# A Trainium2 kernel whose last wait, for all stores, is moved from the sync engine to TensorE

## The chip, the cores and the metric

The kernel runs on one core of one Trainium2 chip. The metric is the device time of one execution in microseconds (us). It covers the program's instructions and something around them: the profiled execution has a time of 46.19 us, and its span, from the first to the last instruction of the kernel, is 44.9 us.

## The reference

64 samples of 64 channels by 512 steps (float32) are each multiplied by one 64 by 64 matrix, picked from a table of 200 by an integer per sample, and the product is added to the sample:

```
w = weights[conditions]                      # (64, 64, 64)
out = x + einsum('bct,bcd->bdt', x, w)       # x, out: (64, 64, 512)
```

## The kernel before

Two samples lie one above the other on the 128 partitions, so there are 32 pairs of 512 columns. The pairs go through the kernel in eight turns of four pairs (1 MB in, 1 MB out a turn). The identity is added to every gathered matrix, so that one product gives `x + x @ w`.

Each engine has its own function, which only lists that engine's instructions in order.

- SyncE (`on_sync`) issues five loads (L94; turns 0, 1, 2, 3 and then 4 to 7 in one of 4 MB), waits until VectorE has moved its part of turns 0 to 2 (L96), and then issues six stores (L101), each behind waits for both engines that write `y_sb` (L98, L99): turns 0 and 1 together, 2 and 3 together, then 4, 5, 6 and 7 one by one. Every store adds 16 to the semaphore `stored` when its bytes have landed. SyncE's last instruction is L102, the wait for `stored` at 96, which is 16 times six.
- TensorE (`on_tensor`) spreads the row numbers (L140), runs ten matmuls on loaded data whose result nobody reads (L146), computes turns 0 to 2 in quadrants (L158), turn 3 with block-diagonal weights (L166), and turns 4 to 7 with the same helper in a loop of two passages (L177) of two turns each. A turn in the loop begins with waits for the data (L179) and the placed weights (L181, L182). The loop is the last thing in TensorE's program.
- ScalarE and VectorE build the weights and move each turn's two products from PSUM to `y_sb` (L117, L216), which raises `moved_by_act` and `moved_by_dve`.
- GpSimd gathers the matrices (L128) and passes the arrival of x on to TensorE (L134).

The framework puts a few instructions ahead of each engine's function, all listed under L235: a DRAIN and a semaphore event per engine, by which the engines start together, and four small memsets on GpSimd. It puts none behind the functions. What the chip does after the last instruction of an engine is in no row.

Of the kernel before, what the change touches and what calls it, by code (L numbers as in the profile page):

```python
# [7 lines left out]
def conditioned_residual_kernel(nc: bass.Bass, x: bass.AP, conditions: bass.AP, table: bass.AP, out: bass.AP):  # L8
# [26 lines left out]
    STORES = [(0, 1), (2, 3), (4, 4), (5, 5), (6, 6), (7, 7)]  # L35

    ctx = ExitStack()
    with ctx:
# [3 lines left out]
        def semaphore(name):  # L42
            return ctx.enter_context(nc.semaphore(name))
# [39 lines left out]
        stored = semaphore("stored")  # L83

        def halves(h):
            return slice(h * C, (h + 1) * C)

        def pairs_of(first, last=None):
            return slice(4 * first, 4 * (first if last is None else last) + 4)

        def on_sync(sp):
            for first, last in LOADS:
                pairs = pairs_of(first, last)
                sp.dma_start(x_sb[:, pairs, :], x[:, pairs, :]).then_inc(x_loaded[first], 16)  # L94

            sp.wait_ge(moved_by_dve, SETS + 1)  # L96
            for first, last in STORES:
                sp.wait_ge(moved_by_act, last + 1)  # L98
                sp.wait_ge(moved_by_dve, last + 1)  # L99
                pairs = pairs_of(first, last)  # L100
                sp.dma_start(out[:, pairs, :], y_sb[:, pairs, :]).then_inc(stored, 16)  # L101
            sp.wait_ge(stored, 16 * len(STORES))  # L102

        def on_scalar(act):
            act.dma_start(condition[:, :, :], conditions).then_inc(condition_loaded, 16)
# [30 lines left out]
        def on_tensor(pe):  # L136

            pe.wait_ge(one_set, 1)
            pe.wait_ge(rows_along, K)
            nc.tensor.matmul(product[0][0][:, 0, 0:1], row_along[:, :, :, :].rearrange("one h k n -> one (h k n)"),  # L140
                             one[:, :], start=True, stop=True).then_inc(rows_spread, 1)

            pe.wait_ge(x_loaded[0], 16)
            pe.wait_ge(x_loaded[1], 16)
            with pe.Fori(0, 5):
                nc.tensor.matmul(product[1][0][:, 0, :], x_sb[:, 0, 0:P], x_sb[:, 0, :], start=True, stop=True)  # L146

            pe.wait_ge(w_ready, 1)
            for turn in range(TILED):
                pe.wait_ge(x_loaded[turn], 16)  # L150
                if turn >= SETS:
                    pe.wait_ge(moved_by_act, turn - SETS + 1)
                    pe.wait_ge(moved_by_dve, turn - SETS + 1)
                for j in range(2):
                    for g in range(2):
                        n = 4 * turn + 2 * j + g
                        for h in range(PAIR):
                            product_of = nc.tensor.matmul(product[turn % SETS][h][halves(g), j, :],  # L158
                                                          w_all[halves(h), :, n], x_sb[halves(h), n, :],
                                                          start=True, stop=True)  # L160
                product_of.then_inc(multiplied, 1)

            def whole_pairs(s, x_pair):
                for j in range(2):
                    for g in range(2):
                        product_of = nc.tensor.matmul(product[s][j][:, g, :], w_diag[:, s, 2 * j + g, :],  # L166
                                                      x_pair(2 * j + g), start=True, stop=True)
                product_of.then_inc(multiplied, 1)

            pe.wait_ge(x_loaded[TILED], 16)
            pe.wait_ge(moved_by_act, TILED - SETS + 1)
            pe.wait_ge(moved_by_dve, TILED - SETS + 1)
            whole_pairs(TILED % SETS, lambda g: x_sb[:, 4 * TILED + g, :])
            pe.wait_ge(moved_by_act, LOOPED - SETS + 1)
            pe.wait_ge(moved_by_dve, LOOPED - SETS + 1)
            with pe.Fori(0, (TURNS - LOOPED) // SETS) as passage:  # L177
                for s in range(SETS):
                    pe.wait_ge(x_ahead, passage * SETS + (s + 1))  # L179

                    pe.wait_ge(placed_by_act, passage * SETS + (s + 1))  # L181
                    pe.wait_ge(placed_by_dve, passage * SETS + (s + 1))  # L182
                    whole_pairs(s, lambda g: x_sb[:, bass.ds(passage * (4 * SETS) + (4 * (LOOPED + s) + g), 1), :])

        def on_vector(dve):
            nc.vector.memset(zero[:, :], 0.0).then_inc(zero_set, 1)
# [27 lines left out]
            for turn in range(TURNS):  # L214
# [3 lines left out]
                if TILED <= turn <= LAST - SETS:  # L218
                    nc.vector.tensor_copy(w_diag[halves(1), turn % SETS, :, D:PAIR * D],  # L219
                                          w_all[halves(1), :, pairs_of(SETS + turn)].rearrange("p d n -> p n d")  # L220
                                          ).then_inc(placed_by_dve, 1)

        on_sync(nc.sync)
        on_scalar(nc.scalar)
        on_gpsimd(nc.gpsimd)
        on_tensor(nc.tensor)
        on_vector(nc.vector)

# [28 lines left out]
```

## Time and profile before

| what | us |
|---|---|
| three runs | 46.01, 46.11, 48.03 |
| median | 46.11 |
| the profiled execution's own time | 46.19 |
| its span | 44.9 |
| its own time less its span | 1.3 |

The rows further down are all of the profiled execution. Engines are PE (TensorE matmuls), PEld (its weight loads), DVE (VectorE), ACT (ScalarE), POOL (GpSimd) and SP (SyncE). A "q" behind a name is the engine's sequencer, which deals with waits, registers, branches and the issue of DMAs. The duration of a wait instruction in these rows is only its execution, once the semaphore has its value; the time before it is in the view of waits.

### The profile page before, as it was taken

How to read it: one execution, taken by the hardware profiler on the slowest of the kernel's cores; microseconds unless marked ns; L12 is line 12 of the kernel's file. 1: busy time of each engine (PE TensorE's matmuls, PEld its weight loads, DVE VectorE, ACT ScalarE, POOL GpSimd, SP SyncE). 2: the span in 40 equal slices, each digit the busy share in tenths (PEclk: the TensorE clock that was granted, in tenths of full speed). 3: DMA queues.
4: the chain of work that ended last, by engine and by line, in shares of the span. 5: the costliest groups of instructions: out<-in, count | busy, mean ns of one | idle time of the engine just before them, and what ended most of it. 6: DMA issues, size and time to landing. Idle time of an engine off the chain costs nothing.

```text
span 44.9 us, 331 instructions
## 1 busy us (share of the span) xinstructions
PE 31.0 (69%) x100; PEld 13.4 (30%) x100; DVE 15.1 (34%) x24; ACT 13.4 (30%) x16; POOL 1.6 (4%) x9
## 2 busy tenths in 40 slices
PE   0040000499999979999999699999999999920000
PEld 0040000433534144543453235344354453300000
DVE  1220000000009990758730490085086073063000
ACT  0894000000000064736710480085085071062000
POOL 4008100000000000000000000000000000000000
PEclk9999999999999999999999999999999999999999
DMA  0389999999999899999995989999998999999993
GB/s 0 81 314 431 424 431 431 424 431 431 416 438 519 372 467 467 467 467 467 438 467 248 438 380 424 409 453 438 424 424 372 409 424 424 431 424 394 402 438 153
DMA packets 1730, 17.83 MB, mean 397 GB/s; under 512 B 194, under 2 KB 194, under 8 KB 194
## 3 DMA queue, kind: packets, MB, share of 16 engines
q1 hardware_dynamic: 1584, 16.78, 89.2%
q0 software_dynamic: 144, 1.05, 5.5%
q10 hardware_dynamic: 2, 0.00, 0.0%
HBM read 9.44 MB, written 8.39 MB: 397 GB/s over the span
## 4 chain that ended last, share of the span: by engine, by line
DMA 50%; PE 31%; SPq 4%; DVE 3%; issue 1%; POOLq 0%
DMA x_sb<-x 50%; PE product L166 31%; SPq L94 4%; DVE y_sb L216 3%; POOLq L134 0%
## 5 line engine op out<-in xcount | busy, mean ns | idle before, releaser
L166 PE MATMUL product<-x_sb,w_diag 128*128 (+1 forms) x40 | 17.7, 597 | 0.4 <-POOLq L134 0.4
L216 DVE COPY y_sb<-product 128x1024 f32<-128x1024 f32 x8 | 9.8, 1224 | 12.9 <-PE product L166 10.5
L117 ACT COPY y_sb<-product 128x1024 f32<-128x1024 f32 x8 | 8.1, 1012 | 13.6 <-PE product L166 11.3
L146 PE MATMUL product<-x_sb 128*128 128x512 f32 x10 | 7.3, 907 | 5.4 <-DMA x_sb<-x 5.4
L166 PEld LDWEIGHTS product<-x_sb,w_diag 128*128 128x128 f32 x40 | 7.4, 190 | 10.5 <-issue 10.5
L158 PE MATMUL product<-x_sb,w_all 64*64 64x512 f32 x48 | 5.5, 601 | 0.3 <-DVE w_all L205 0.3
L146 PEld LDWEIGHTS product<-x_sb 128*128 128x128 f32 x10 | 2.9, 302 | 9.1 <-issue 9.1
L111 ACT COPY w_diag<-w_all 64x256 f32<-64x256 f32 x1 | 0.6, 642 | 12.3 <-DVE w_all L205 12.3
L202 DVE TENSOR_TENSOR gathered<-gathered,piece 128x64 f32<-128x64 f32 x1 | 0.3, 267 | 10.2 <-DMA gathered<-weights,table_row 10.2
L158 PEld LDWEIGHTS product<-x_sb,w_all 64*64 64x64 f32 x48 | 2.5, 200 | 3.3 <-issue 2.1
L205 DVE STREAM_TRANSPOSE w_all<-gathered 128x2048 f32<-128x2048 f32 x1 | 2.3, 2311 | 0.0
L140 PE MATMUL product<-one,row_along 1*128 1x1 f32 x2 | 0.6, 342 | 2.5 <-DVE row_along L193 2.5
L120 ACT COPY w_diag<-w_all 64x256 f32<-64x256 f32 x3 | 1.9, 633 | 0.0
L108 ACT ACT_TABLE_LOAD x1 | 1.3, 1283 | 1.3 <-PEq L235 1.3
L219 DVE COPY w_diag<-w_all 64x256 f32<-64x256 f32 x3 | 1.2, 410 | 0.1
L108 ACT COPY w_diag<-zero 64x512 f32<-64x512 f32 x2 | 1.2, 616 | 0.0
L140 PEld LDWEIGHTS product<-one,row_along 1*128 1x128 f32 x2 | 0.5, 304 | 2.5 <-issue 2.5
L128 POOL DMA_INDIRECT gathered<-weights,table_row x1 | 1.1, 1068 | 2.3 <-DVE table_row L196 2.3
L113 ACT COPY w_diag<-w_all 64x256 f32<-64x256 f32 x1 | 0.6, 642 | 0.0
L193 DVE TENSOR_SCALAR row_along<-condition 1x64 f32<-1x64 int32 x2 | 0.3, 178 | 0.8 <-DMA condition<-conditions 0.8
L209 DVE COPY w_diag<-w_all 64x256 f32<-64x256 f32 x1 | 0.4, 401 | 0.0
L196 DVE CAST table_row<-product 128x1 int32<-128x1 f32 x1 | 0.2, 158 | 0.7 <-PE product L140 0.7
(9 smaller groups left out, 1.6 us busy)
## 6 DMA issues: line engine op xcount, KB each, us to landing
x_sb<-x SPq DMA_DIRECT2D x4, 1024.0 KB, 9.3
x_sb<-x SPq DMA_DIRECT2D x1, 4096.0 KB, 22.7
out<-y_sb SPq DMA_DIRECT2D x2, 2048.0 KB, 8.0
out<-y_sb SPq DMA_DIRECT2D x4, 1024.0 KB, 5.4
condition<-conditions ACTq DMA_DIRECT2D x1, 0.2 KB
gathered<-weights,table_row POOLq DMA_INDIRECT x1, 9.8
```

Of the source, the lines that this page charges most:

```text
L94: sp.dma_start(x_sb[:, pairs, :], x[:, pairs, :]).then_inc(x_loaded[first], 16)
L108: nc.scalar.copy(w_diag[halves(h), :, :, (1 - h) * D:(2 - h) * D].rearrange("p s n d -> p (s n) d"), zero[halves(h), :].unsqueeze(2).to_br ...
L117: nc.scalar.copy(y_sb[:, 4 * turn:4 * turn + 2, :], product[turn % SETS][0][:, :, :]).then_inc(moved_by_act, 1)
L120: nc.scalar.copy(w_diag[halves(0), turn % SETS, :, 0:D], w_all[halves(0), :, pairs_of(SETS + turn)].rearrange("p d n -> p n d")).then_inc( ...
L128: nc.gpsimd.indirect_dma_start(gathered[:, :], None, table, bass.IndirectOffsetOnAxis(ap=table_row[:, 0:1], axis=0)).then_inc(w_gathered, 16)
L140: nc.tensor.matmul(product[0][0][:, 0, 0:1], row_along[:, :, :, :].rearrange("one h k n -> one (h k n)"), one[:, :], start=True, stop=True ...
L146: nc.tensor.matmul(product[1][0][:, 0, :], x_sb[:, 0, 0:P], x_sb[:, 0, :], start=True, stop=True)
L158: product_of = nc.tensor.matmul(product[turn % SETS][h][halves(g), j, :], w_all[halves(h), :, n], x_sb[halves(h), n, :], start=True, stop= ...
L166: product_of = nc.tensor.matmul(product[s][j][:, g, :], w_diag[:, s, 2 * j + g, :], x_pair(2 * j + g), start=True, stop=True)
L205: nc.vector.transpose(w_all[:, :, :], gathered[:, :].rearrange("p (d c) -> p d c", d=D)).then_inc(w_ready, 1)
L216: nc.vector.tensor_copy(y_sb[:, 4 * turn + 2:4 * turn + 4, :], product[turn % SETS][1][:, :, :]).then_inc(moved_by_dve, 1)
L219: nc.vector.tensor_copy(w_diag[halves(1), turn % SETS, :, D:PAIR * D], w_all[halves(1), :, pairs_of(SETS + turn)].rearrange("p d n -> p n ...
```

## The change

The wait for `stored` at 96 is taken out of SyncE's program, where it is the last instruction, and put at the end of TensorE's, behind the loop. Nothing else is touched.

```diff
@@ on_sync
                 pairs = pairs_of(first, last)
                 sp.dma_start(out[:, pairs, :], y_sb[:, pairs, :]).then_inc(stored, 16)
-            sp.wait_ge(stored, 16 * len(STORES))
@@ on_tensor
                     pe.wait_ge(placed_by_act, passage * SETS + (s + 1))
                     pe.wait_ge(placed_by_dve, passage * SETS + (s + 1))
                     whole_pairs(s, lambda g: x_sb[:, bass.ds(passage * (4 * SETS) + (4 * (LOOPED + s) + g), 1), :])
+            pe.wait_ge(stored, 16 * len(STORES))
```

## Rows read from the trace of the kernel before

**Rows 1.** The page's 40 slices of the span: busy tenths and granted clock

```profile
PE   0040000499999979999999699999999999920000
DVE  1220000000009990758730490085086073063000
ACT  0894000000000064736710480085085071062000
PEclk9999999999999999999999999999999999999999
DMA  0389999999999899999995989999998999999993
```

**Rows 2.** Chain that ended last, its last pieces: start us, us, what

```profile
25.55 0.03 POOLq L134
25.57 14.01 PE product L166 x32
39.58 0.02 issue
39.60 1.22 DVE y_sb L216
```

**Rows 3.** Waits of SP's queue: us in total, times, longest

```profile
SPq L99 <- DVE y_sb L216: 33.9, 6, 17.9
SPq L102 <- DMA out<-y_sb: 3.6, 1, 3.6
```

**Rows 4.** Timeline from 39 us to the end: start us, us, engine, line

```profile
39.60 1.01 ACT L117 COPY y_sb<-product 128x1024 f32<-128x1024 f32 x1 [2.42 <-PE product L166]
40.90 0.33 SPq L101 DMA_DIRECT2D out<-y_sb  x1
```

**Rows 5.** L101, the stores' issue, and its time to landing

```profile
L101 SPq DMA_DIRECT2D out<-y_sb x6: 332/332/347, 22.9 to 40.9; - x6
DMA to landing us min/median/max: 3.9/6.4/8.6
```

**Rows 6.** Wait instructions L102 (SP), L99 (SP), L182 (PE), L144 (PE): duration ns, starts

```profile
L102 SPq EVENT_SEMAPHORE  x1: 17/17/17, 44.9 to 44.9; - x1
...
L99 SPq EVENT_SEMAPHORE  x6: 17/17/28, 21.2 to 40.9; - x6
...
L182 PEldq EVENT_SEMAPHORE  x4: 51/51/51, 23.2 to 34.4; - x4
...
L144 PEldq EVENT_SEMAPHORE  x1: 51/51/51, 8.3 to 8.3; - x1
```

**Rows 7.** L177, the loop's own instructions on PE's sequencer: duration ns, first and last start

```profile
L177 PEldq FUSED_REGOPS  x2: 50/50/50, 23.1 to 28.0; - x2
L177 PEldq ALU_OP  x2: 32/32/32, 27.6 to 35.1; - x2
L177 PEldq COMPARE_BRANCH  x2: 76/142/209, 27.7 to 35.2; - x2
L177 PEldq MOVE  x1: 33/33/33, 23.0 to 23.0; - x1
```

**Rows 8.** Windows: stretch, us, busy (x instructions), granted PE clock, DMA share, GB/s

```profile
41.24:44.87 3.63, 0.00 (x0) 0.00 (x0) 0.00 (x0) 0.00 (x0) 0.00 (x0) 0.99 0.81 334
44.87:46.40 1.53, 0.00 (x0) 0.00 (x0) 0.00 (x0) 0.00 (x0) 0.00 (x0) 0.50 0.00 0
46.30:46.50 0.20, 0.00 (x0) 0.00 (x0) 0.00 (x0) 0.00 (x0) 0.00 (x0) 0.66 0.00 0
...
46.44:47.00 0.56, 0.00 (x0) 0.00 (x0) 0.00 (x0) 0.00 (x0) 0.00 (x0) 1.00 0.00 0
```

**Rows 9.** L235, the framework's opening instructions by engine: duration ns, starts

```profile
L235 POOLq EVENT_SEMAPHORE  x2: 17/17/17, 0.6 to 0.6; - x2
L235 SPq DRAIN  x1: 7/7/7, 0.0 to 0.0; - x1
L235 DVEq DRAIN  x1: 10/10/10, 0.1 to 0.1; - x1
L235 ACTq DRAIN  x1: 8/8/8, 0.1 to 0.1; - x1
L235 POOLq INC_SWDGE_SEM  x1: 31/31/31, 0.1 to 0.1; - x1
L235 POOL MEMSET const-float32-0.0<- x1: 104/104/104, 0.2 to 0.2; 128x1 f32 x1
L235 PEldq DRAIN  x1: 8/8/8, 0.3 to 0.3; - x1
L235 SPq EVENT_SEMAPHORE  x1: 17/17/17, 0.7 to 0.7; - x1
L235 PEldq EVENT_SEMAPHORE  x1: 51/51/51, 0.7 to 0.7; - x1
```

## The prediction

> **What bounds the kernel now.** I read the page's slices first. They show the DMA engines busy in nearly every slice from 3 to 39, TensorE busy up to slice 36 and idle in the last four [rows 1]. So the last part of the span belongs to the stores. The chain that ended last gives its steps: the arrival of x is passed on at 25.55 us, TensorE's products run from 25.57 to 39.58, VectorE's last copy from 39.60 to 40.82 [rows 2]. The timeline then has the last store, issued at 40.90 and done with issuing at 41.23 [rows 4], and the waits of SP's queue close it: the wait at L102 stood 3.6 us until that store had landed [rows 3], which is the landing of 3.9 us after its issue, the shortest of the six [rows 5]. L102 itself starts at 44.9 and takes 17 ns; it is the last instruction of the span [rows 6].
>
> None of this is touched. The change moves no load, matmul, copy or store, only the instruction that stands behind the last landing. It can therefore change three things: how soon that instruction runs once the last bytes are there, how long it takes, and what lies between it and the end of the measured time, about which the profile says little. I sum against the profiled execution: 46.19 us, of which 44.87 is the span and 1.32 lies around it. It is 0.08 above the median of the runs, 46.11.
>
> **How much lies behind the wait.** The windows behind the span carry no instruction, but they have a granted clock until a certain point: 0.50 from 44.87 to 46.40, 0.66 as the mean from 46.30 to 46.50, and 1.00 from 46.44 on, where nothing is recorded any more [rows 8]. For the mean of 0.66, x of the 0.20 us must be at 0.50 and the rest at 1.00: x = 0.2 * 0.34 / 0.5 = 0.136. The record ends at 46.44. The first busy instruction of the program, GpSimd's memset, starts at 0.2 to 0.25 [rows 9], and 46.44 - 0.25 = 46.19, the execution's own time. That is a fit and no proof, but I take it: all of the time outside the span lies behind the wait, 46.44 - 44.87 = 1.57 us. I call it the tail. It is an estimate, and it bounds from above what can be won, since no other cost is in reach of the change.
>
> **The change part by part.**
>
> *SP loses L102.* Its last instruction is then the issue that ends at 41.23 [rows 4], 3.6 us before the last landing [rows 3]. Whatever SP does for itself at the end of a program now lies beside the last store, which moves 334 GB/s in that stretch with all engines idle [rows 8]. It is cover of 3.63 us for a tail of 1.57, more than enough.
>
> *TensorE gets a wait.* Nothing is queued behind it in TensorE's program, and no engine waits for anything that comes after it. Its sequencer reaches it early: the loop's last ALU_OP and branch start at 35.1 and 35.2 [rows 7], while the matmuls already handed over run on to 39.58 [rows 2]. An instruction of the sequencer does not hold up matmuls in front of it, as the four waits at L182 show: the last starts at 34.4 [rows 6] in the midst of slices at 90% [rows 1]. Its cost there is nothing, hidden by the last matmuls and then by the last store. If that cover were gone it would be one instruction of 51 ns.
>
> *The wake-up.* A wait on SP takes 17 ns, on PE 51 [rows 6], so the span ends 34 ns later. How long each takes to notice a landing has no row good to a few ns. POOL's 25.55 reaches PE's matmul at 25.57 with its own 0.03 in it [rows 2]; the start releases SP and PE alike at 0.7 [rows 9]. The bounds are 0 and 0.03, and I take 0.01. Together the span gets 0.04 to 0.05 longer: 44.92.
>
> *The tail with PE as the last to arrive.* The trace doesn't show this part, so it is bounded from both sides. If the tail is the same whoever comes last, the cost is zero. If it is all SP's own work, it goes beside the last store and 1.57 is won. If it is work that each engine does for itself, PE does it more slowly: its sequencer starts MOVE, FUSED_REGOPS and a wait at 23.0, 23.1 and 23.2 [rows 6, 7], 0.1 us apart, while SP has a wait and the start of the store's issue between the copy's end at 40.82 and 40.90 [rows 2, 4], 0.04 apart. At 0.06 more an instruction, a tail of 1.57 that holds 1.57 / 0.04 = 39 of SP's instructions would be 2.3 longer. So the ends are -1.57 and +2.3. The value that I take is zero to +0.1, say +0.01, by the nearest row: at the only point where all engines meet, the start, SP and PE are released in the same tenth of a microsecond [rows 9], which speaks for a meeting that hardly depends on who it is.
>
> The sum: 46.19 + 0.034 + 0.01 + 0.01 = 46.24 on the profiled execution's scale, 46.16 on the scale of the median. I forecast 46.2, no change that can be seen; 2% of this kernel is 0.92 us, about what a measurement of it can tell from no change.
>
> One rule speaks against the change. In the opening rows the engines do not begin together: SP's DRAIN starts at 0.0, those of DVE and ACT at 0.1, PE's at 0.3 [rows 9]. The Trainium skill, page "Runtime: NRT & Kernel Launch", section "The ~15µs preamble/postamble breakdown", says that the runtime's barriers go from engine to engine and back, eight hops of 44 ns over five engines. An engine at the head of such a line that comes last pays eight hops, one at its far end four. If PE is the head, as its late start would fit, the page would make the time an estimated 4 * 44 = 176 ns longer: 46.4. The order of the starts agrees with a line of that sort, but a different amount of work ahead of the DRAINs would look the same. The same table gives the barrier behind a kernel about 1.5 us; the tail of 1.57 from the windows is that long, and no row here shows what is in it.
>
> **The rivals.**
>
> *A: the line of engines (0.3 us).* By rows alone: PE starts 0.3 after SP [rows 9]. If this order is that of a line in which word is passed on, and the last to arrive must pass it the long way, then the end is later by up to the same 0.3, so 46.5; if the line runs the other way round, earlier by as much, 45.9. For it: the stagger. Against it: at 0.7 both are released at once. Either way it is within 2%.
>
> *B: SP's own work at the end is hidden.* For it: SP has issued eleven DMAs and has their queue to look after, and it is free from 41.23. Against it: no row shows any such work, and TensorE must have an end of its own, which now comes last. If half of the tail is SP's and PE has nothing like it, 46.19 - 0.78 + 0.04 = 45.4; if all of it, 44.7. It is faster by over 2% when SP's share exceeds PE's by 0.96 us, some 60% of the tail.
>
> *C: TensorE's own end is dearer, the other side.* In the kernel before, TensorE is through with its program by 39.6 at the latest [rows 2] and does whatever it has to do at the end beside the last copies and the last store, at a granted clock of 0.99 to 1.00 [rows 1, 8]. In the kernel after it does so behind the last landing, with nothing beside it. The price is 0.06 us for each instruction that both have, by the pace above. If half of the tail is such work, 20 instructions, 1.2 us: 47.4; if all, 48.5. It decides from 15 instructions on (15 * 0.06 = 0.9). The clock is at 0.50, which is 1.2 GHz, in the stretch behind the span, after TensorE has been idle since 39.58 [rows 2, 8]; if the sequencer's pace hung on it, each instruction would cost yet more. For it: the pace of PE's sequencer, 51 ns against 17. Against it: the common release at the start.
>
> *D: the move does nothing.* Should the end of the program wait for the DMA queue on SP in any case, SP stays the last and PE's wait runs beside it: 46.19 to 46.24.
>
> **How the numbers follow.** The forecast has 0.40, with a range of its own of 46.0 to 46.5. A has 0.15, B 0.22, C 0.18, D 0.05. Of B somewhat more than half, 0.12, is beyond 2% (below 45.2); of C half, 0.09, is beyond 47.0. That leaves 0.79 within 2%. The range that should hold the time 8 times in 10 reaches well into B and C: 45.1 to 47.1, with about 0.11 below and 0.08 above.
>
> **What would show it right or wrong.** The last instruction of the changed profile must be a semaphore event of 51 ns on PE's sequencer, and its wait must name the stores as its releaser; its length is from 35.3 to 44.9, over 9 us, and costs nothing. SP's last row must be the issue at 40.9. Everything up to 40.9 must be as before, the last landing again 3.9 us after its issue; the span must be 44.9. If the difference between the execution's own time and its span stays at 1.3, forecast and D hold; 1.0 or 1.6 is A; 0.9 or less is B; 1.9 or more is C. The forecast would be wrong if the own time moved by more than 0.3 while the span did not, for then the tail depends on who comes last; it would be wrong in another way if the last store itself landed at another time, which none of the cases has a reason for.

## The result and the profile after

| | before | after |
|---|---|---|
| median us | 46.05 | 46.34 |
| runs, lowest to highest us | 18, 45.81 to 48.03 | 18, 46.18 to 46.60 |
| profiled execution: own time, us | 46.19 | 46.43 |
| its span, from the trace, us | 44.87 | 44.84 |
| own time less span, us | 1.32 | 1.59 |

The ratio of after to before is 1.0066 with a 95% interval of 1.0051 to 1.0081. The changed kernel is slower by 0.3 us: well within 2%, but clear of the noise. Executions far above their fellows, like the one of 48.03 us, are left out of every ratio. The profiled execution's span is even 0.03 us shorter than before.

The page of the changed kernel begins with its span and its slices; these lines answer to [rows 1]:

```profile
span 44.8 us, 331 instructions
...
PE   0040000499999369999999699999999999920000
...
PEclk9999999999999999999999999999999999999975
DMA  0679999999999799999995999899998999999993
```

The pattern at the end is that of before: DMA up to slice 39, TensorE idle in the last four. Only the granted clock is lower in the last two slices. The timeline from 40 us on shows the same end as [rows 2, 4], 0.04 to 0.05 us earlier throughout:

```profile
39.56 1.01 ACT L116 COPY y_sb<-product 128x1024 f32<-128x1024 f32 x1 [2.42 <-PE product L165]
39.56 1.23 DVE L216 COPY y_sb<-product 128x1024 f32<-128x1024 f32 x1 [2.21 <-PE product L165]
40.86 0.33 SPq L101 DMA_DIRECT2D out<-y_sb  x1
```

The waits of SP's queue, answering to [rows 3], have lost the one at L102. The wait is now L183, on TensorE's sequencer, as its own row has it, and the stores still land 3.9 us after their issue at best, as in [rows 5]. The three fences are the view of waits, line L183 and line L101:

```profile
SPq L99 <- DVE y_sb L216: 33.9, 6, 17.9
SPq L101 <- DVE y_sb L216: 1.7, 1, 1.7
SPq L235 <- PEq L235: 0.7, 1, 0.7
```

```profile
L183 PEldq EVENT_SEMAPHORE  x1: 51/51/51, 44.8 to 44.8; - x1
```

```profile
L101 SPq DMA_DIRECT2D out<-y_sb x6: 332/332/348, 22.8 to 40.9; - x6
...
DMA to landing us min/median/max: 3.9/6.4/8.6
```

So nothing inside the span explains 0.3 us. The windows behind the span show where it went, in the same view as [rows 8] (columns: stretch, its length, the five engines, granted clock, DMA share, GB/s):

```profile
44.87:46.40 1.53, 0.00 (x0) 0.00 (x0) 0.00 (x0) 0.00 (x0) 0.00 (x0) 0.50 0.00 0
46.30:46.50 0.20, 0.00 (x0) 0.00 (x0) 0.00 (x0) 0.00 (x0) 0.00 (x0) 0.50 0.00 0
46.50:47.00 0.50, 0.00 (x0) 0.00 (x0) 0.00 (x0) 0.00 (x0) 0.00 (x0) 0.82 0.00 0
```

Before, the mean of 0.66 between 46.30 and 46.50 put the end of the clock's record at 46.44. Here the record goes on at 0.50 past 46.50; a mean of 0.82 over the next 0.50 us means that 0.5 * 0.18 / 0.5 = 0.18 of it are at 0.50, so it ends at 46.68. Less the first memset at 0.25 that is 46.43, which again is the execution's own time. The estimate by which the prediction placed everything outside the span behind the last wait holds for the second kernel too. The traces also hold exact times in nanoseconds (ns): the last store's last landing is at 44838 before and 44762 after, the record ends at 46435 and 46676. From landing to end it is 1.597 us before and 1.914 after, 0.317 more. Of these, 12 ns are the wake-up (16 ns from landing to the start of the wait instruction on SP, 28 on TensorE), 34 ns the instruction's longer duration, and 271 ns lie behind the last instruction of the kernel.

A profile shows one execution. The times of all executions carry it as well, since each is given with its span: own time less span is 1.58 us on average over the 18 runs after, and 1.31 over 28 runs of the kernel before beside the first experiments. The spread (standard deviation) is about 0.03 us, a tenth of the difference.

### The profile page after: what moved, and what is told of

Same layout as the page of the kernel before. It is cut to its first block, busy times and chain, and to the rows that moved or that the text cites. A ratio compares the mean times of both kernels' runs of the same rounds, so it can differ in the third digit from the quotient of the medians.

```text
span 44.8 us, 331 instructions
## 1 busy us (share of the span) xinstructions
PE 30.2 (67%) x100; PEld 13.0 (29%) x100; DVE 15.0 (34%) x24; ACT 13.4 (30%) x16; POOL 1.6 (4%) x9
## 4 chain that ended last, share of the span: by engine, by line
DMA 50%; PE 31%; SPq 4%; DVE 3%; issue 1%; POOLq 0%
DMA x_sb<-x 50%; PE product L165 31%; SPq L94 4%; DVE y_sb L216 3%; POOLq L133 0%
## 5 line engine op out<-in xcount | busy, mean ns | idle before, releaser
L145 PE MATMUL product<-x_sb 128*128 128x512 f32 x10 | 6.6, 820 | 5.5 <-DMA x_sb<-x 5.5
```

## The experiments

The question: why does the same end of the data path cost 0.27 us more, behind the last instruction, when TensorE is last to arrive? Everything here is a change of who waits, of what follows the wait, or of what goes before it.

### Each engine in turn

All of these take the wait out of `on_sync` and append it to another function:

```diff
-            sp.wait_ge(stored, 16 * len(STORES))
+            act.wait_ge(stored, 16 * len(STORES))     # e1, at the end of on_scalar
+            dve.wait_ge(stored, 16 * len(STORES))     # e2, at the end of on_vector
+            pool.wait_ge(stored, 16 * len(STORES))    # e3, at the end of on_gpsimd
```

Expected of ScalarE:

> ScalarE waits for the stores instead of TensorE. Two theories of the 0.3 us that TensorE costs as the last to arrive. Line: the engines take their closing turns in the order in which their DRAINs start (SP 0.00, DVE 0.12, ACT 0.13, POOL 0.13, PE 0.32 us), and what an engine costs as the last follows that order: ACT some 0.1 over SP, 46.15. Pace: each engine has closing instructions of its own, and their pace is that of its waits (17 ns on ACT as on SP, 51 on PE): ACT costs what SP does, 46.05. Third theory, early SP: what costs is that SP is through with its program 3.6 us before the end, whoever waits: then 46.34 here too.

Expected of VectorE:

> VectorE waits for the stores. Line: 46.15, like ACT, as its DRAIN starts 0.12 us after SP's. Pace: its wait takes 21 ns against SP's 17, so 46.05 to 46.1. Early SP: 46.34.

Expected of GpSimd:

> GpSimd waits for the stores. Line: 46.15 to 46.2, between ACT and PE. Pace: its wait takes 17 ns, as SP's: 46.05. Early SP: 46.34.

And with two engines waiting, where the kernel before keeps its wait and only `pe.wait_ge(stored, 16 * len(STORES))` is added:

> SP keeps its wait and TensorE has one too. If TensorE's late arrival is what costs (line or pace), the time is that of the changed kernel, 46.34. If SP's early end is what costs, SP is no longer early and the time is that of the kernel before, 46.05.

What was measured, in us. The fourth column is the mean over the runs (12 of each kernel, 6 of GpSimd's), the last is from the one profiled execution's trace:

| who waits | median | ratio (interval) | own time less span | landing to end |
|---|---|---|---|---|
| SP (before) | 46.10 | | 1.31 | 1.597 |
| VectorE | 46.22 | 1.0009 (0.9987 to 1.0031) | 1.42 | 1.688 |
| ScalarE | 46.27 | 1.003 (1.0005 to 1.0055) | 1.48 | 1.742 |
| TensorE (after) | 46.34 | 1.0066 (1.0051 to 1.0081) | 1.58 | 1.914 |
| GpSimd | 46.68 | 1.0128 (1.0093 to 1.0163) | 1.85 | 2.140 |
| SP and TensorE | 46.43 | 1.0058 (1.0035 to 1.008) | 1.57 | 1.912 |

(The TensorE row and its ratio are of the 18 runs of the result; the other ratios are against the SP row.) VectorE's ratio by itself cannot be told from 1; its 0.11 us shows only in the fourth column, where the spread is 0.03. The wait instruction itself is 17 ns long on SP, ScalarE and GpSimd and 21 on VectorE, as the rows of the three lines show, of ScalarE's, VectorE's and GpSimd's kernel in this order:

```profile
L122 ACTq EVENT_SEMAPHORE  x1: 17/17/17, 45.2 to 45.2; - x1
```

```profile
L221 DVEq EVENT_SEMAPHORE  x1: 21/21/21, 44.8 to 44.8; - x1
```

```profile
L134 POOLq EVENT_SEMAPHORE  x1: 17/17/17, 44.6 to 44.6; - x1
```

Three things follow. First, each engine has a price as the last to arrive, in the order SP, VectorE, ScalarE, TensorE, GpSimd, and the times from landing to end order them as the averages do. Second, early SP is out: SP was just as early in all of e1 to e3, but they cost from 0.1 to 0.5, and with both waiting SP is not early and the cost is TensorE's to 2 ns (1.912 against 1.914). These two rows of the kernel in which both wait show both woken at the same landing:

```profile
L102 SPq EVENT_SEMAPHORE  x1: 17/17/17, 44.8 to 44.8; - x1
```

```profile
L184 PEldq EVENT_SEMAPHORE  x1: 51/51/51, 44.8 to 44.8; - x1
```

Third, neither theory of the order is right as it was stated (what each had right is seen further down, in the steps behind the last instruction). "Pace" by the length of a wait wanted ScalarE and GpSimd to cost what SP does; they cost 0.17 and 0.54 us more. "Line" by the order of the opening DRAINs wanted VectorE, ScalarE and GpSimd within a few hundredths of each other; GpSimd costs about 0.4 more than the other two. (The first expectation dates GpSimd's DRAIN at 0.13 us. What starts there is its INC_SWDGE_SEM; its DRAIN starts at 0.31, just ahead of TensorE's at 0.32.)

### The pace of each engine's waits

A wait of 17 ns may still be followed late by the next instruction. Four kernels put 16 more waits behind the last one, for a semaphore that has long had its value:

```diff
+            pe.wait_ge(stored, 16 * len(STORES))
+            for _ in range(16):
+                pe.wait_ge(w_ready, 1)
```

TensorE with these lines, SP (where the extra waits are for `moved_by_dve`), GpSimd and ScalarE:

> The changed kernel with 16 more waits behind TensorE's last one, for semaphores that have long had their value. Pace theory: what an engine costs as the last to arrive is its closing instructions at its own pace, the same number for each. The 16 waits measure the pace on TensorE, the rows give it directly: I expect 0.09 to 0.1 us each, 1.5 us in all, so 47.9. What lies behind the span should stay at 1.83 us. If TensorE's 0.27 us over SP behind the span is so many instructions times the difference in pace, some 4 or 5 of them do it at 0.06.

> The kernel before with 16 more waits behind SP's last one. The pace on SP: 0.04 us each, 0.65 in all, so 46.75. What lies behind the span stays at 1.56.

> GpSimd waits for the stores and then 16 times more. GpSimd has cost most as the last (0.54 us over SP from the landing to the end). Pace theory: its pace must then be slower than TensorE's, over 0.1 us an instruction, 1.6 in all and more: 48.3 or later. Rival: GpSimd has a dear instruction of its own in its closing, of the kind of its opening DRAIN (203 ns against 7 to 10 on the others); then its waits come at the pace of its two opening events, 0.08 us, 1.25 in all: 47.9.

> ScalarE waits for the stores and then 16 times more. ScalarE has cost 0.145 us over SP from the landing to the end. Pace theory, with TensorE's 0.32 at a pace 0.06 slower than SP's: ScalarE's pace must lie about half way between, 0.07 us, 1.1 in all: 47.3. If its pace is SP's 0.04, pace is not what sets the cost of an engine as the last, and its place in a line or something of its own does.

The times are misses, all four: 46.56, 45.97, 46.34 and 46.23 us in one run each, beside 46.09 for the kernel before, nowhere near the 0.65 to 1.6 us more. The rows of the extra waits' lines say why; they are of TensorE's, SP's, GpSimd's and ScalarE's kernel in this order (columns: count, duration in ns least/median/most, first and last start in us):

```profile
L185 PEldq EVENT_SEMAPHORE  x9: 51/51/8656, 35.5 to 36.4; - x9
```

```profile
L104 SPq EVENT_SEMAPHORE  x9: 17/28/3073, 41.1 to 41.6; - x9
```

```profile
L136 POOLq EVENT_SEMAPHORE  x9: 17/43/18447, 25.4 to 26.0; - x9
```

```profile
L124 ACTq EVENT_SEMAPHORE  x9: 17/38/4635, 39.5 to 40.1; - x9
```

### The granted clock

The clock is 0.50 behind the span in both kernels, which is 1.2 GHz. If TensorE's sequencer ran at half pace with it, closing late would be dear for that reason. The first test writes the wait for the stores itself 17 times, so that nine instructions must follow the landing:

```diff
+            pe.wait_ge(stored, 16 * len(STORES))
+            for _ in range(16):
+                pe.wait_ge(stored, 16 * len(STORES))
```

> The changed kernel with its last wait written 17 times in all; two conditions share one instruction, so 9 instructions follow the landing. With 16 redundant waits ahead of the landing TensorE's instructions of this kind came 0.106 us apart at a granted clock of 1.0, SP's 0.061. Clock theory: behind the landing, at a clock of 0.5, they come 0.2 apart: the span grows by 1.6. Rival: 0.106 apart at either clock; the span grows by 0.85, the whole to 47.2, and 1.80 to 1.83 stay behind the span.

The line's row, and the windows around it:

```profile
L185 PEldq EVENT_SEMAPHORE  x9: 51/51/51, 44.7 to 45.6; - x9
```

```profile
43.00:44.00 1.00, 0.00 (x0) 0.00 (x0) 0.00 (x0) 0.00 (x0) 0.00 (x0) 0.50 0.97 401
44.60:45.60 1.00, 0.00 (x0) 0.00 (x0) 0.00 (x0) 0.00 (x0) 0.00 (x0) 0.50 0.00 0
```

Nine instructions take from 44.7 to 45.6, 0.9 us, at a clock of 0.50. At a clock of 1.00 the nine of the kernel with 16 more waits on TensorE started from 35.5 to 36.4, the same 0.9. In the trace seven of the eight steps are 105 or 106 ns and one is 136. From the landing to the end of the last it is 0.956 us against 0.079 in the changed kernel, 0.88 more where 0.85 was expected; the time is 47.16 (47.2 expected) and 1.80 us lie between the last instruction and the end of the clock's record. The pace of the sequencer's waits, 106 ns, is the same at both clocks.

The second test keeps TensorE at work while the last store is under way:

```diff
+            pe.wait_ge(moved_by_act, TURNS)
+            pe.wait_ge(moved_by_dve, TURNS)
+            for _ in range(4):
+                nc.tensor.matmul(product[1][0][:, 0, :], x_sb[:, 0, 0:P], x_sb[:, 0, :], start=True, stop=True)
+            pe.wait_ge(stored, 16 * len(STORES))
```

> The changed kernel, but TensorE runs four more matmuls, whose results nobody reads, between the last copies at 40.8 us and the landing at 44.8, before it waits for the stores. Clock theory: TensorE's closing is dear because it is carried out at a granted clock of 0.5 after a stretch of idleness; with the engine at work until 44.3 the clock behind the span should be 1.0, and the time from the landing to the end should fall from 1.91 to about SP's 1.6, the whole to 46.05. Rival (the sequencer's pace has nothing to do with that clock): 1.91 and 46.34, whatever the clock. If the clock is 0.5 behind the span all the same, the run tells nothing of it.

The median is 46.57, the ratio 1.0135 (1.0084 to 1.0186). The windows show the matmuls and a clock of 1.00 to the end:

```profile
41.00:44.60 3.60, 3.60 (x8) 1.36 (x8) 0.00 (x0) 0.00 (x0) 0.00 (x0) 1.00 0.80 328
44.70:47.20 2.50, 0.00 (x0) 0.00 (x0) 0.00 (x0) 0.00 (x0) 0.00 (x0) 1.00 0.05 20
47.32:48.80 1.48, 0.00 (x0) 0.00 (x0) 0.00 (x0) 0.00 (x0) 0.00 (x0) 1.00 0.00 0
```

The profiled execution is one of the two far above the rest (48.61 and 48.87), and its last store landed at 47.24, but what lies behind the last instruction can be read from it: own time 48.87 less a span of 47.32 is 1.55 us, as in the changed kernel, not the 1.3 that the clock theory wanted. One reservation: this trace has no record of the clock at all, so its 1.00 is the view's reading of nothing recorded, and the run alone would be weak. It agrees with the nine waits. The run brought a cost of its own too: the other five times average 46.62 with own time less span between 1.56 and 2.3, up to 0.7 more than after. Its page has a DMA row that neither the page of before nor that of after has, a fetch of instructions of 16 KB on queue 8:

```profile
q8 instruction: 1, 0.02, 0.1%
```

The trace places it at 43.0 us, while the last store moves. That it is the cause of the extra time was not tested.

### Beside each other, or one behind the other

If the engines first meet and then close together, an engine's price might be paid on top of the others' lateness. Both wait here, and SP goes through eight more waits for the same value:

```diff
             sp.wait_ge(stored, 16 * len(STORES))
+            for _ in range(8):
+                sp.wait_ge(stored, 16 * len(STORES))
@@ on_tensor
+            pe.wait_ge(stored, 16 * len(STORES))
```

> SP and TensorE both wait for the stores, and SP then goes through 8 more waits in 4 instructions, so it is through some 0.24 us after the landing. Beside-each-other theory: each engine has its own way from its last instruction to the common end, TensorE's is 0.27 to 0.3 longer than SP's, and the longest decides: SP's 0.24 are free, 1.91 from the landing to the end as with both waiting. In-series theory: the closing comes after a common meeting, and a later SP puts all of it later: 2.15.

```profile
L104 SPq EVENT_SEMAPHORE  x5: 17/28/28, 44.9 to 45.2; - x5
```

```profile
L186 PEldq EVENT_SEMAPHORE  x1: 51/51/51, 44.9 to 44.9; - x1
```

TensorE is through at 44.998 and SP only at 45.209, 0.26 us later than with a single wait. From the landing to the end it is 1.882 us, against 1.912 with both at one wait. SP's 0.26 us cost nothing; had they been paid on top, it would have been 2.17. The two ways run beside each other and the longer decides: TensorE's 44.998 + 1.83 is 46.83, SP's 45.209 + 1.56 is 46.77, and the record ends at 46.80.

The traces show why. Besides instructions they hold the time of every semaphore update. One semaphore, number 2, is named by no instruction of the kernel, nor by the opening ones of L235, whose events work on 96 and 97. It is updated 18 times at the end of every program, in two groups of nine. Each group is a line of steps. In the changed kernel the first group stands wholly behind the last instruction: its first step is 187 ns after that instruction's end, and the other eight follow at 34, 38, 44, 23, 97, 39, 36 and 46 ns, 357 in all.

In the kernel before, four of the nine are over before SP is done, at 39738, 40724, 40763 and 40974 ns. They fit the ends of the other engines: the first is 172 ns after TensorE's last product, the second 109 after ScalarE's last instruction, the third 39 after the second (GpSimd has long been idle), the fourth 145 after VectorE's last copy. Only five steps are left behind SP. So word goes from TensorE over ScalarE, GpSimd and VectorE to SP and back, and an engine that is last holds up all steps from its own on. The traces give a semaphore and a time, not the engine that made the step; the order is read from these counts and times:

| last to arrive | steps behind its last instruction | its last instruction to its step, ns | its step to the ninth, ns | both | over SP |
|---|---|---|---|---|---|
| SP | 5 | 111 | 162 | 273 | |
| VectorE | 6 | 140 | 242 | 382 | 109 |
| GpSimd | 7 | 552 | 285 | 837 | 564 |
| ScalarE | 8 | 118 | 324 | 442 | 169 |
| TensorE | 9 | 187 | 357 | 544 | 271 |

Within 0.03 us the last column gives the prices of 0.11, 0.54, 0.17 and 0.27 us that the averages over the runs show. What follows the ninth step does not depend on the engine: 784 to 819 ns, in which some 200 other semaphores are updated once each, then the second line of nine steps, 357 or 358 ns, and 114 to 119 to the end of the clock's record.

So TensorE's 271 ns are 195 of the line, which it starts and which turns round at SP, and 76 of its own before its step. GpSimd stands in the middle of the line; it is dear for its 552 ns (548 in the trace with 16 more waits). In the run with SP late, SP's step was due at 45209 + 111 = 45320, and it came at 45324, as the line reached it: its lateness was covered, with 4 ns to spare. With the four extra matmuls TensorE's two parts are 186 and 358 ns in the one trace, as in the changed kernel; what made others of its executions dearer is not in them as far as this shows.

### A version that might beat both

SP has the lowest price of the five, so only its own 0.033 us from landing to the end of its instruction could be shortened. With 16 redundant waits it was 0.022 and the whole 1.557. The smallest such kernel has one redundant wait ahead of the last, which the compiler joins with it:

```diff
+            sp.wait_ge(moved_by_dve, TURNS)
             sp.wait_ge(stored, 16 * len(STORES))
```

> The kernel before with one redundant wait ahead of SP's last one, so that one instruction carries both conditions. With 16 such waits the time from the landing to the end was 1.557 us against 1.597. If the joint instruction is the reason, 1.56 here and 46.01 in all, 0.04 (0.1%) faster than before; if it was chance, 1.60 and 46.05.

The ratio is 1.0005 (0.999 to 1.0021), median 46.06 against 46.03 of the kernel before on the same chip, and 1.587 us from landing to end. The joint instruction was woken at the landing as before and took 28 ns. Of the 0.040 us that the kernel with 16 waits was ahead, 0.032 lie between the two lines (787 ns against 819), a stretch that is 784 to 792 in some traces and 815 to 819 in others, whoever is last. So it was mostly chance. Nothing tried is faster than the kernel before.

## Why the prediction was right, and where it was not

The time, 46.34, lies in the range and near the forecast of 46.2, and "within 2%" was the likeliest case. But the forecast was no change to speak of, and there is one of 0.3 us that its own range, 46.0 to 46.5, merely contains. That the range holds the time is due to the smallness of the term that it missed, which is luck. By its steps:

- *Nothing inside the span moves.* Right: the last store issued 0.05 us earlier, landing 3.9 us after its issue again, spans of 44.87 and 44.84.
- *TensorE's sequencer reaches the wait early, at no cost.* Right: 35.5 us, as the nine waits show. The forecast had 35.3.
- *The wake-up: 34 ns for the instruction and 10 for the noticing.* Right: 34 and 12.
- *All that lies outside the span lies behind the wait, 1.57 us.* It held in each trace with a record of the clock: its end less the first memset is the execution's own time, for example 46.68 - 0.25 = 46.43.
- *The tail with TensorE last: +0.01.* This is the step that failed. The term is 0.27 us. It was taken from the opening rows, where SP and TensorE are released at the same 0.7 [rows 9]. That row shows how soon an engine is let go, and in a meeting on two other semaphores (96 and 97) than the line behind the kernel. What was wanted is how much an engine has before it between its last instruction and the end: 544 ns up to the ninth step for TensorE, 273 for SP. The mark that the prediction set for it decided well: own time less span, "1.3, forecast and D hold; 1.0 or 1.6 is A"; it is 1.59 in the profiled execution.
- *Rival A, 0.3 us by the line of engines.* Right in mechanism, sign and size. It gave 46.5 on the profiled execution's scale, where 46.43 was measured, and the last to arrive does pass word the long way: 357 ns of steps behind TensorE's, 162 behind SP's. The 195 ns between them are most of the 271. The other 76 are TensorE's own part before its step, which A did not have. The stagger of the opening DRAINs is a poor guide to the order: by first instruction it is 0.12 us over SP for VectorE, 0.13 for ScalarE and GpSimd and 0.32 for TensorE, and GpSimd's price is 0.54. The section "The ~15µs preamble/postamble breakdown" of the Trainium skill's "Runtime: NRT & Kernel Launch" gives the line ahead of a kernel eight hops of 44 ns, an estimate of 0.18 us for four of them. The trace agrees: eight steps behind the kernel take 357 ns, 45 each, and the four more that TensorE's place has over SP's took 139; the other 56 of the 195 are on the way back, nearly all at the turn at SP (97 ns against 43 where SP is last). By that estimate the prediction had 46.4, its nearest number to 46.43. But its remark that the tail of 1.57 us is as long as one barrier of that table does not hold: 1.56 is two lines, the stretch of 0.8 between them and the rest.
- *Rival B, SP's own closing work is hidden.* Its size was far off: SP's own part is 111 ns, not half of the tail. It is hidden in the changed kernel, but TensorE's 187 stand in its place, so the end is soonest with SP last.
- *Rival C, TensorE's own end is dearer.* Its sign was right: TensorE's own part is 76 ns longer than SP's. Its price, 1.2 us or more, was far off, since it took half of the tail for work paid at TensorE's pace. Its clause on the clock finds no support: the nine waits are as fast at 0.50, and in the kernel before TensorE's step comes 172 ns after its last matmul (whose end is modelled) at a clock of 1.00, against 187 after its wait at 0.50.
- *Rival D, the move does nothing.* Refuted by the 0.27 us.

What stays open is what an engine does in its own part, the 111 to 552 ns between its last instruction and its step, and above all why GpSimd's is 552. No instruction is recorded there. Nor is it known what made the kernel with four more matmuls dearer in some of its executions.

## What to carry to other kernels

In this kernel the end of the program has a price by engine: the last wait belongs on SP, where the line turns round and which has the shortest part of its own, and above all not on GpSimd, for up to 0.54 us. It matters only for kernels of some tens of microseconds. When a change touches the last instruction, the span says nothing of it: compare own time less span over all runs, whose spread of 0.03 us resolves what the medians barely do.

## What the runs showed of the hardware that was not expected

- From the landing of the last store to the end of the measured time it is 1.60 us with SP as the last to arrive, 1.69 with VectorE, 1.74 with ScalarE, 1.91 with TensorE and 2.14 with GpSimd.
- Behind the last instruction nine steps on one semaphore go from TensorE over ScalarE, GpSimd and VectorE to SP and back, 357 ns for the eight hops, and they start before the slower engines are done. Each engine adds a part of its own before its step: SP 111 ns, ScalarE 118, VectorE 140, TensorE 187, GpSimd 552. A second line of 357 ns follows 0.8 us later.
- TensorE's sequencer goes through waits 106 ns apart, at a granted clock of 1.00 and of 0.50 alike; SP's, ScalarE's and GpSimd's are 61, 75 and 84 ns apart on average.
- Consecutive waits end up in pairs in one instruction, not in the order in which they are written, and a wait that is a second condition shows as the duration of the instruction (8656 ns on TensorE). Such a row is no work.
